# A fused attention and expert kernel: the cross-attention context taken relative to its last token, and keys projected for two batches at a time

## The reference, cut to what matters

```python
# cross-attention: query = layernorm(x), key = value = ctx_1024 (128, 257, 256)
q = split_heads(query @ Wq.T + bq)
k = split_heads(ctx @ Wk.T + bk)
v = split_heads(ctx @ Wv.T + bv)
attn = softmax(q @ k.T)                  # over the 257 context tokens
x = x + (attn @ v) @ Wo.T + bo
x = x + self_attention(layernorm(x))     # RMS norm, rope, sigmoid weights
x = x + experts(layernorm(x))            # 8 experts, capacity 160, argmax routing
```

## Time and profile before

| | |
|---|---|
| median of 3 runs | 1346.71 us (1345.29 to 1346.93) |
| the profiled execution | 1344.86 us |
| its span, first to last instruction | 1343.0 us |
| mean granted TensorE clock | 0.970 of full |
| one tile in the steady part | 36.7 us |
| busy in 600 to 1150 us (550 us) | TensorE 490.6, VectorE 429.9, ScalarE 395.0, GpSimd 260.0 us |

### The profile page before, as it was taken

How to read it: one execution, slowest core, us unless ns; L and a number is a source line. 1 busy time by engine, 2 the same in 40 slices (tenths; PEclk the granted TensorE clock), 3 DMA queues, 4 the chain that set the end, 5 groups by cost and what they waited for, 6 DMA issues and landing times.

```text
span 1343.0 us, 37302 instructions
## 1 busy us (share of the span) xinstructions
PE 1157.5 (86%) x14033; PEld 936.5 (70%) x14033; DVE 945.0 (70%) x2523; ACT 872.4 (65%) x2443; POOL 569.7 (42%) x1045
## 2 busy tenths in 40 slices
PE   6898889888888898889888888988898888864797
PEld 5676777767767777777767767767777677742697
DVE  3667777777777777777777777877777777763121
ACT  3676767777777667767777777667677777632131
POOL 1244454455444444444454444444444554431121
PEclk9899999999999999999999999999999999975899
DMA  6414211111211111111111111111111111000474
GB/s 148 126 47 144 84 57 43 51 54 51 52 40 45 49 52 47 50 47 39 46 48 50 49 30 50 49 49 46 50 40 39 48 48 45 14 9 13 115 225 153
DMA packets 71904, 81.93 MB, mean 61 GB/s; under 512 B 16987, under 2 KB 50732, under 8 KB 71728
## 3 DMA queue, kind: packets, MB, share of 16 engines
q1 hardware_dynamic: 65280, 75.19, 19.3%
q0 software_dynamic: 3200, 3.71, 0.8%
q10 hardware_dynamic: 3248, 0.66, 0.2%
HBM read 64.79 MB, written 16.56 MB: 61 GB/s over the span
## 4 chain that ended last, share of the span: by engine, by line
DVE 33%; PE 31%; ACT 20%; issue 9%; POOL 6%; SPq 0%; DVEq 0%; DMA 0%; ACTq 0%; POOLq 0%
ACT prob L739 8%; ACT wbd L799 4%; PE score L444 4%; PE vps L411 4%; PE kps L401 4%; DVE prob L974 4%; ACT qz L728 3%; DVE nmx L963 3%; PE shared L477 3%; PE shared L532 3%; PE shared L523 3%; PE score L670 3%; PE score L684 3%; DVE pr L1116 3%; POOL ctx_p L1273 2%
## 5 line engine op out<-in xcount | busy, mean ns | idle before, releaser
L739 ACT ACTIVATE prob<-score,nmx 128x257 f32<-128x257 f32 x512 | 236.2, 476 | 175.8 <-DVE nmx L963 175.0
L401 PE MATMUL kps<-ctx_p,wk_p 128*128 128x256 f32 x1536 | 213.6, 289 | 0.2 <-POOL ctx_p L1273 0.2
L411 PE MATMUL vps<-wv_p,ctx_p 128*128 128x256 f32 x1536 | 212.7, 288 | 0.0
L1273 POOL TENSOR_TENSOR ctx_p<-ctxT,ctx_p 128x512 fp32r<-128x512 f32 x128 | 152.1, 1188 | 119.8 <-ACT ctx_p L755 119.8
L411 PEld LDWEIGHTS vps<-wv_p,ctx_p 128*128 128x128 f32 x1536 | 192.6, 192 | 12.4 <-issue 12.4
L401 PEld LDWEIGHTS kps<-ctx_p,wk_p 128*128 128x128 f32 x1536 | 195.4, 192 | 5.4 <-issue 2.3
L963 DVE TENSOR_REDUCE nmx<-score 128x2 f32<-128x514 f32 x256 | 163.1, 679 | 15.7 <-PE score L428 15.7
L1291 POOL TENSOR_TENSOR plast<-const,prob 128x128 f32<-128x128 f32 x128 | 64.1, 501 | 257.7 <-DVE prob L974 257.7
L974 DVE TENSOR_SCALAR prob<-prob,rsum 128x257 f32<-128x257 f32 x512 | 158.3, 352 | 9.0
L444 PE MATMUL score<-const,prob 128*128 128x128 f32 x1024 | 145.7, 280 | 7.5 <-DVE prob L974 3.5
L444 PEld LDWEIGHTS score<-const,prob 128*128 128x128 f32 x1024 | 114.1, 142 | 44.4 <-DVE prob L974 28.6
(11 more groups left out here) (163 smaller groups left out, 2188.4 us busy)
## 6 DMA issues: line engine op xcount, KB each, us to landing
ctxT<-in_ctxT SPq DMA_DIRECT2D x128, 257.0 KB, 3.0
w<-in_w SPq DMA_DIRECT2D x16, 1024.0 KB, 9.7
xq<-in_x SPq DMA_DIRECT2D x32, 128.0 KB, 3.3
xr<-in_x SPq DMA_DIRECT2D x32, 128.0 KB, 2.5
qbd<-qkT SPq DMA_DIRECT2D x256, 16.0 KB, 1.8
out<-row SPq DMA_DIRECT2D x32, 128.0 KB, 1.9
slots<-row SPq DMA_DIRECT2D x10, 257.0 KB, 5.6
x_a<-slots SPq DMA_DIRECT2D x8, 129.0 KB, 2.1
```

The source lines that it names most:

```text
L401: last = mm(kps[:, c, :], wk_p[:, x, n, c * P:(c + 1) * P], ctx_p[:, g, y, n, :], start=(n, x) == (0, LO), stop=(n, y) == (C - 1, LO))
L411: last = mm(vps[:, c, :], ctx_p[:, g, x, n, c * P:(c + 1) * P], wv_p[:, y, n, :], start=(n, x) == (0, LO), stop=(n, y) == (C - 1, LO))
L739: last = af(prob[:, m, :], score[:, m, 0:S], ACT.Exp, bias=nmx[:, m:m + 1], scale=1.0, accum_out=esum[:, m:m + 1])
L1273: g.tensor_tensor(ctx_p[:, g_, LO, :, :], ctxT[:, r, :, g_, 0:SM], ctx_p[:, g_, HI, :, :].bitcast(F32), ALU.subtract).then_inc(s["ctx_part ...
```

## The change

The context minus its last token is computed on GpSimd in a new step `context_sub`, for two batches at once (1024 elements a row), in place in `ctxT`. `context_hi` and `context_lo` also take two batches at once, so they run at `j` = 1 and 3 only, and `context_sub` for the next tile at `j` = 0 and 2. `ctx_p` and `kT` grow to hold two groups of two batches. TensorE's `keys` works on one half of the output features for two batches, 6 matmuls of 512 columns per `j`, and ScalarE copies them with one instruction. `kT`'s last column is filled with `bk` once. `last_key`, `last_prob`, `last_probs`, the multiplication by the last values and `attended` are gone. In exchange `extract` starts on VectorE with an instruction that was ScalarE's (`even_heads`, L720), which now also adds the last token's value plus bias. `scores2` moves from place (0, 1) to (0, 0). `normalise` scales 256 columns rather than 257. At the start, the last values are computed at `j` = 0 of the first iteration, and the last tokens are loaded ahead of `Wv`.

```diff
 # TensorE
-            def keys(t, j):
-                for c in range(C):
-                    for n in range(C):
-                        for x, y in PASSES:
-                            last = mm(kps[:, c, :], wk_p[:, x, n, c * P:(c + 1) * P], ctx_p[:, g, y, n, :],
+            def keys(t, r, c):
+                pe.wait_ge(s["ctx_parts"], 2 * t + r + 1)
+                pe.wait_ge(s["k_evac"], 4 * t + 2 * r + c)
+                for n in range(C):
+                    for x, y in PASSES:
+                        last = mm(kps[:, :, :], wk_p[:, x, n, c * P:(c + 1) * P], ctx_p[:, r, y, n, :, :],
-                    (0, 0): s1 and (lambda: (turn("att_tmp", t1 + 1), last_probs(t1))),
-                    (0, 1): lambda: (t3 is not None and positions(t3),
-                                     s2 and (turn("relu_done", t2 + 1), scores2(t2))),
-                    (0, 2): s1 and (lambda: (turn("x1_step", 3 * t1 + 1), project_out(att, wo, "att_done", t1, "o1_ps"))),
+                    (0, 0): s2 and (lambda: (turn("relu_done", t2 + 1), scores2(t2))),
+                    (0, 1): t3 is not None and (lambda: positions(t3)),
+                    (0, 2): (s1 and (lambda: (turn("x1_step", 3 * t1 + 1),
+                                              project_out(att, wo, "ext_step", 2 * t1 + 2, t1, "o1_ps")))
+                             or once(i) and (lambda: (turn("vlast_done", C), last_rows()))),
-                    if ahead:
-                        keys(ta, ja)
+                    if xa and (j < 2 or q):
+                        keys(i + j // 2, 1 - j // 2, j % 2)
 # ScalarE
-                for c in range(C):
-                    last = af(kT[:, j % 2, c, 0:SM], kps[:, c, :], ACT.Identity, bias=b_k[:, c:c + 1], scale=1.0)
+                af(kT[:, r, c, :, 0:SM], kps[:, :, :], ACT.Identity, bias=b_k[:, c:c + 1], scale=1.0).then_inc(s["k_evac"], 1)
+            def context_hi(t, r):
+                act.wait_ge(s["ctx_sub"], 2 * t + r + 1)
+                af(ctx_p[:, r, HI, :, :, :], ctxT[:, r, :, :, 0:SM], ACT.Copy).then_inc(s["ctx_hi"], 1)
-                        even_heads(att, gather[:, :, 0, :], "pv_done", TB * (t1 + 1), "ext_step")
+                    if q and j % 2:
+                        context_hi(i + 1, j // 2)
 # VectorE
             def extract(t):
+                v.scalar_tensor_tensor(att[:, :, :].rearrange("p c (j q) -> p c j q", j=TB),
+                                       gather[:, :, 0, :].rearrange("p c (j q) -> p c j q", j=TB), k["even"],
+                                       vlast[:, t, :, :].unsqueeze(3).to_broadcast([P, C, TB, L]), ALU.mult, ALU.add
+                                       ).then_inc(s["ext_step"], 1)
                 dve.wait_ge(s["ext_step"], 2 * t + 1)
-            def attended(t):
-            def last_values(t):
 # GpSimd
-            def last_key(t, j):
-            def last_prob(t, j):
+            def context_sub(t, r):
+                pool.wait_ge(ctx_in[r], 16 * C * (t + 1))
+                g.tensor_tensor(ctxT[:, r, :, :, 0:SM], ctxT[:, r, :, :, 0:SM],
+                                lastT[:, :, b:b + 2].unsqueeze(3).to_broadcast([P, C, 2, SM]), ALU.subtract
+                                ).then_inc(s["ctx_sub"], 1)
...
+                    if q and j % 2:
+                        context_lo(i + 1, j // 2)
+                    if q and j % 2 == 0:
+                        context_sub(i + 1, j // 2)
 # SyncE
-                sp.wait_ge(s["ctx_parts"], floor0(TB * t + 2 * r - 2))
+                sp.wait_ge(s["ctx_parts"], floor0(2 * t + r - 1))
```

More of the change, by code:

```diff
@@ L365, in last_rows @@
             def last_rows():
-                pe.wait_ge(s["wk_in"], 16 * 4)
                 pe.wait_ge(s["wv_in"], 16)
-                pe.wait_ge(s["wkv_in"], 16 * 6)
+                pe.wait_ge(s["last_in"], 16)
                 for c in range(C):
                     for n in range(C):
-                        mm(shared[:, c * P:(c + 1) * P], wk[:, n, c * P:(c + 1) * P], lastT[:, n, :],
-                           start=n == 0, stop=n == C - 1)
-                for c in range(C):
-                    for n in range(C):
-                        last = mm(shared[:, (C + c) * P:(C + c + 1) * P], wv[:, n, c * P:(c + 1) * P], lastT[:, n, :],
-                                  start=n == 0, stop=n == C - 1)
+                        last = mm(sh_c[:, c], wv[:, n, c * P:(c + 1) * P], lastT[:, n, :], start=n == 0, stop=n == C - 1)
                 last.then_inc(s["last_ps"], 1)
@@ L429, in scores @@
                                   qz[rows, half, e, j, :, :].rearrange("p h q -> p (h q)"),
-                                  kT[rows, b_slot(j), e, :], start=True, stop=True)
+                                  kT[rows, j // 2, e, j % 2, :], start=True, stop=True)
                         if e and m % 2:
@@ L463, in weighted_values, with project_out @@
                 last.then_inc(s["pv_done"], 1)
[L465 to L475, removed]
+            def project_out(x, w, ready, count, t, done):
+                pe.wait_ge(s[ready], count)
                 for c in range(C):
@@ L569, in _ @@
             project_queries(0)
-            turn("vlast_done", 1)
-            last_rows()
             pe.wait_ge(s["wparts_done"], 2)
-            keys(0, 0)
+            for c in range(C):
+                keys(0, 0, c)
             values(0, 0)
@@ L704, in _ @@
             load_paired(act, wk, a["Wk"], "wk_in")
-            for dst, src, done in ((wv[:], a["Wv"], "wv_in"), (lastT[:], a["lastT"], "wkv_in")):
+            for dst, src, done in ((lastT[:], a["lastT"], "last_in"), (wv[:], a["Wv"], "wv_in")):
                 act.dma_start(dst, src.rearrange("(c p) n -> p c n", c=C)).then_inc(s[done], 16)
@@ L815, in _ @@
             queries(0, 0)
-            act.wait_ge(s["wkv_in"], 16 * 6)
             context_hi(0, 0)
-            act.wait_ge(s["last_ps"], 1)
-            for c in range(C):
-                last = af(klast[:, c, :], shared[:, c * P:(c + 1) * P], ACT.Identity, bias=b_k[:, c:c + 1], scale=1.0)
-            last.then_inc(s["klast_done"], 1)
+            act.wait_ge(s["wkv_in"], 16 * 5)
+            keys(0, 0, 0)
             context_hi(0, 1)
-            keys(0, 0)
+            keys(0, 0, 1)
             values(0, 0)
@@ L870, in body @@
                         sigmoid_exp(t2)
-                    if xa and j == 3 and q:
-                        context_hi(i + 1, 1)
                     if j == 0 and q:
@@ L973, in normalise @@
                         m = 2 * c + g
-                        last = v.tensor_scalar(prob[:, m, :], prob[:, m, :], rsum[:, m:m + 1], None, ALU.mult)
+                        last = v.tensor_scalar(prob[:, m, 0:SM], prob[:, m, 0:SM], rsum[:, m:m + 1], None, ALU.mult)
                     last.then_inc(s["norm_done"], 1)
@@ L1158, in body @@
                         norm_x(1)
-                    if j == 0 and s1:
-                        last_values(t1)
                     if j == 1 and s1:
@@ L1210, in body @@
                         setup(j)
+                    if j == 0 and once(i):
+                        last_values()
             tiles(body)
@@ L1354, in _ @@
             power("q", "xn_stat", 3, 0, "xn_pow")
+            context_sub(0, 0)
             context_lo(0, 0)
+            context_sub(0, 1)
             context_lo(0, 1)
-            pool.wait_ge(s["klast_done"], 1)
-            last_key(0, 0)
             def body(i, half):
@@ L1363, in body @@
                 for j in range(TB):
-                    if xa and (j < TB - 1 or q):
-                        last_key(*((i, j + 1) if j < TB - 1 else (i + 1, 0)))
                     if j == 0 and once(i):
@@ L1373, in body @@
                         rows_parts(t1)
-                    if xa:
-                        last_prob(i, j)
                     if j == 1 and s1:
                         rms(t1)
-                    if xa and (j < 2 or q):
-                        context_lo(*((i, j + 2) if j < 2 else (i + 1, j - 2)))
+                    if q and j % 2:
+                        context_lo(i + 1, j // 2)
+                    if q and j % 2 == 0:
+                        context_sub(i + 1, j // 2)
                     if j == 0 and s1:
```

104 lines of the change are left out of this document (38 added, 66 removed).

## The result

The changed kernel takes 1456.33 us in the median of 4 runs (1452.32 to 1463.8), the kernel before 1346.15. The ratio is 1.0825, 95% interval 1.0779 to 1.0871: 8% slower. The forecast was 1432 in a range from 1372 to 1462. The profiled execution of the changed kernel is its slowest, 1463.8 us with a span of 1462.0.

What follows compares the result with a forecast made beforehand. The prediction took a ring of dependent steps on several engines, not TensorE, as the bound. Its terms, 25 + 16 - 7 + 51 - 1.5 + 2 = +85.5 us, gave 1432 us, range 1372 to 1462.

Steps and rivals of the forecast that it cites:

- covers that fail: Rival: the held L974 at j = 0 and late low part at j = 1 add 30 us, 1462 us; chance 0.12.
- What bounds the kernel: Whole tile, 36.74 us: a ring of dependent steps on several engines, with TensorE behind in few places despite 86% busy.
- GpSimd's durations: `context_lo` and `context_sub`: 1024 elements take 2.11 us each, where 512 took 1.188.
- L1116 at j = 3: Routing's scaling of 8 columns, held by GpSimd's low part: ends 0.86 us later in 29 iterations, +25 us.
- L974 at j = 2: Normalisation on VectorE, held by GpSimd's `context_sub`: 1.7 us later a tile, +51 us; lower bound zero.
- `extract`: Start of j = 0: one more VectorE instruction ahead of the maxima, 0.52 us a tile, +16 us, bounds 12 to 19.
- The key copy: ScalarE at j = 0: one copy of 512 columns for two, 0.49 us rather than 0.71, -7 us.
- The covers at j = 0 and j = 1: Held L974 at j = 0 and later low part at j = 1 cost zero; without cover up to 30 and 9 us.
- The keys: TensorE at j = 3: 6 matmuls of 512 columns gain nothing over 12 of 256, +2 us, bounds -2 and +4.
- TensorE's busy time: Profile after the change: TensorE busy less, by about 32 us, with more idle.
- The start: First keys wait for one more `context_sub` and longer parts, but last-token matmuls no longer precede: zero, bounds 0 and +3.5 us.
- the wait of `context_sub` for its DMA: GpSimd at j = 0, with `power` queued behind: zero, since the context load goes out many us ahead.

Runs made afterwards that it cites:

- e8: The kernel before, without TensorE's last-token work and the VectorE instructions behind it, leaving out the last token's share and bias: 1339.57 us, ratio 0.9954.
- e4: The kernel before, with only GpSimd's low part of j = 3 held back until the routing's one-hot is written: 1319.05 us, ratio 0.9811.
- e2: The changed kernel, with GpSimd's low part of j = 3 held back until the routing has written its one-hot: 1384.7 us, ratio 1.0303.
- e1: The changed kernel, with GpSimd's subtraction of j = 2 held back until VectorE has applied the tile's second norm: 1404.76 us, ratio 1.0441.
- e5: The changed kernel, with each GpSimd subtraction and low part issued as two instructions of 512 elements rather than one of 1024: 1436.3 us, ratio 1.0684.
- e7: e3 with even heads extracted on ScalarE again, leaving out the last token's value and its bias: 1333.63 us, ratio 0.9904.
- e9: e3 with TensorE's keys as 12 matmuls of 256 columns rather than 6 of 512: 1345.34 us, ratio 1.0003.
- e3: The changed kernel with both waits, those of e1 and e2 together: 1343.06 us, ratio 0.9986.
- e11: e3 with the last values computed ahead of the two large memsets of the first iteration, on VectorE: 1339.47 us, ratio 0.9957.

## Why the prediction was right

Slower, in the range, and for the reason given; 1432 was 24 us too low. That the number came so close is in part luck. The tile was forecast some 16 us too dear over the run (85 against 69 us at equal clock), and about 50 us of clock and start, which the sum did not have, came on top. The upper bound of 1462 stood for another cause, covers that fail, and those held. By its steps:

- *What bounds the kernel.* The ring and not TensorE: shown by e8 (5.5 us for all of TensorE's last-token work) and e4.
- *GpSimd's durations.* 2.11 us forecast; the low part takes 2.18, the subtraction 1.99 in the mean.
- *L1116 at j = 3.* 0.86 later forecast, 0.92 measured in the median. e2 shows that the hold is the cause.
- *L974 at j = 2.* This was the term without a row, and I took its upper end, 1.7. The pair is 1.44 longer, and e1 takes 1.34 from the tile. By the rule in the Trainium skill, "SBUF — State Buffer", section "Who interferes with whom", VectorE in its double-rate mode and GpSimd share a pair of ports, and whichever starts first keeps it for the whole instruction. The runs agree: e1 frees L943 by moving GpSimd's instruction alone, and in e5 the hold lasts for one GpSimd instruction.
- *`extract`.* 0.52 forecast, 0.40 by e7.
- *The key copy.* -0.22 forecast. The next instruction starts 0.57 us after it (710.00 to 710.57), not 0.49, against 0.71 before, so 0.14 came. L770, from which the 0.49 was read, is a copy without a bias; the key copy adds one.
- *The covers at j = 0 and j = 1.* They held. At j = 0 TensorE waited for the ReLU, and at j = 1 the low part ended at 646.34, where the keys started at 647.19 without a wait.
- *The keys.* +2 us forecast with bounds -2 and +4. e9 gives about -2, between -4 and 0. The 12 matmuls of 1.59 us in the earlier trace rows are those of j = 2; at j = 3, where the term counts, they took 1.67 before and the 6 take 1.64.
- *TensorE's busy time.* 32 us less forecast, 9 more measured. In e3, with the clock back, it is 26 less.
- *The sum per tile* was 2.9 us in the forecast and 2.46 at equal clock.

Two terms were mis-sized, and for the total they outweigh the 0.4 us a tile:

- *The start.* The step "I take zero, bounds 0 and +3.5" failed, and it named the wrong place: the first keys start 0.5 us earlier than before. The first scores start 4.9 us later, at 26.97 rather than 22.11, because they now stand behind the keys of two batches, twice the matmul columns, with the copy of the first half between. Each of the two groups of 6 also takes 2.90 us, where it takes 1.64 later; why is not shown. Before, and after:

```profile
18.47 2.28 PE L401 MATMUL kps<-ctx_p,wk_p 128*128 128x256 f32 x12
...
22.11 0.69 PE L428 MATMUL score<-kT,qz 32*64 32x257 f32 x16
```
```profile
17.99 2.90 PE L391 MATMUL kps<-ctx_p,wk_p 128*128 128x512 f32 x6 [4.89 <-issue]
...
21.80 2.90 PE L391 MATMUL kps<-ctx_p,wk_p 128*128 128x512 f32 x6 [0.92 <-ACT kT L727]
...
26.97 0.69 PE L419 MATMUL score<-kT,qz 32*64 32x257 f32 x16
```

  Then `last_values` behind two memsets held TensorE; by e11 the scores behind it start 5.5 us earlier without that, and the run takes 4 us less. Another piece lies in the fourth iteration. The prediction took the wait of `context_sub` for its DMA, with the power queued behind it, at zero, since the load goes out many us ahead. In the steady part it does (issued at 675.65 for the subtraction at 708.23). Here it stood in SyncE's queue behind the expert weights and went out at 144.11, with the DMA engines still full of them (busy share 1.0 to 1.1):

```profile
152.44 1.90 POOL L1236 TENSOR_TENSOR ctxT<-ctxT,lastT 128x1024 f32<-128x1024 f32 x1 [9.03 <-DMA ctxT<-in_ctxT]
...
154.88 0.41 DVE L990 TENSOR_SCALAR y<-x,mv,rstd 128x256 f32<-128x256 f32 x1 [3.25 <-POOL rstd L1228]
...
155.44 0.41 PE L465 MATMUL score<-const,y 128*128 128x128 f32 x2 [2.70 <-DVE y L990]
```

  The iteration lasts 41.93 us, 5.2 more than before, where the tiles behind it are 2.5 to 3.7 longer. With the holds of the steady part gone this wait shows in full: in e3 it is 10.0 us, and the iteration is 5.7 longer than the others. No run moves this load, so the piece is read from the trace and not shown by an experiment. The forecast counted the work moved away from the start, and not whom its new place holds up.
- *The clock.* Not in the sum at all, about 29 us. In 16 tiles, after TensorE's idle stretch at j = 2, the granted clock goes to 0.5, its lower level of 1.2 GHz, for about 3.4 us; in 9 it does so after the idle stretch at j = 0. Three stretches of 4 us of the changed kernel:

```profile
613.00:617.00 4.00, 3.72 (x57) 2.23 (x57) 1.92 (x6) 1.63 (x3) 0.56 (x1) 0.59 0.01 2
640.00:644.00 4.00, 2.71 (x37) 1.73 (x40) 1.95 (x5) 3.93 (x10) 3.05 (x5) 1.00 0.03 9
654.00:658.00 4.00, 3.76 (x56) 2.49 (x57) 2.19 (x7) 1.44 (x3) 0.56 (x1) 0.59 0.04 8
```

In the first and third TensorE transposes, weighs and scores at 0.59, on the chain. A forecast that adds idle time to TensorE has to ask for this. When both holds go (e3), or the one at j = 3 alone (e2), the clock comes back by itself; with the one at j = 2 gone (e1) it comes back in 16 tiles of 28. Five tiles with the same idle stretches kept their clock, and why those did is not shown.

What stays open: how the pieces of the start add up to the 21 us, and what the clock alone is worth, since both attempts to keep it up cost more than they gave.

## What to carry to other kernels

Ask of every long GpSimd instruction which VectorE instructions run beside it: a scaling of 8 columns can last as long as 1024 GpSimd elements. The trace shows it as a minimum far below the median, with both ends together. A wait that puts the GpSimd work behind the short VectorE steps can be worth more than the work that was saved; here one wait took 1.9% off the kernel before and two took 7.8% off the changed one. Joining instructions saves little where columns set the time, makes longer holds, and at the start makes the first result wait for the work of two.

## What the hardware showed that was not expected

- Splitting the holder in two does not halve the cost where the held instructions come in pairs: 1.99 us against 2.06 for the L943 pair (e5).
- TensorE work off the ring is nearly free: 8 matmul instructions and a wait of 1.14 us, with VectorE's three instructions behind them, were worth 0.12 us a tile (e8).
- A ScalarE copy of 512 columns from PSUM with a bias took 0.701 us, where a plain copy takes 0.597. With 256 columns it is 0.492 (L748) against 0.384 (L715) before, so the 0.1 us goes with the bias and not with the length.
